# A two-layer gated network on one core: the hand-written slot tables of the first full turn are changed

## The reference, cut to what matters

```python
q = batch_norm(x1 @ w_q)                            # x1 is the output of the attention
sim = einsum('pbnhd,hkpd->pbnhk', q, keys)          # 8 heads, 2 halves, 32 keys each
sx, ix = top_k(sim[0], 8);  sy, iy = top_k(sim[1], 8)
scores, pk = top_k(sx[..., :, None] + sy[..., None, :], 8)
h = gelu(einsum('bnd,bnhkd->bnhk', x1, down_embed[indices]))
out = einsum('bnhk,bnhkd->bnd', softmax(scores) * h, up_embed[indices])
x2 = x + out
# second layer: h1 = relu(x2n @ W1 + b1); h2 = relu(h1 @ W2 + b2); c = sum_e cw_e (h2 @ W3 + b3)
# then gelu(c @ W1f + b1f) @ W2f + b2f, weighted by the two best of 8 sigmoid gates, and x3 = x2 + that
```

## Time and profile before

| what | value |
|---|---|
| median of 3 runs | 784.82 us (784.77 to 787.23) |
| profiled execution, its own time | 787.02 us |
| its span | 785.2 us |
| PE busy | 741.9 us (94%) |
| DVE busy | 557.1 us (71%) |
| ACT busy | 575.6 us (73%) |
| POOL busy | 312.2 us (40%) |
| mean granted clock of TensorE | 0.987 |

### The profile page before, as it was taken

One profiled execution on the slowest core, in us unless ns is written; L12 is line 12 of the kernel. 1 busy time (PEld: TensorE's weight loads), 2 busy tenths in 40 slices (PEclk: granted clock), 3 DMA queues, 4 the chain that ended last, 5 costly groups with the idle time before them and its releaser, 6 DMA issues.

```text
span 785.2 us, 14852 instructions
## 1 busy us (share of the span) xinstructions
PE 741.9 (94%) x5314; PEld 654.1 (83%) x5314; DVE 557.1 (71%) x1495; ACT 575.6 (73%) x1001; POOL 312.2 (40%) x214
## 2 busy tenths in 40 slices
PE   6889998979878999999999999999999999999998
PEld 4666767869766799899989989999898899999887
DVE  4887888477379877976977797688679756833422
ACT  3677777369797778978987886897889788553243
POOL 2122222179977175344717543572645161000000
PEclk9999999989997999999999999999999999999999
DMA  8940000000000000000000000000000000000000
GB/s 313 333 117 2 3 1 2 1 1 1 1 1 1 1 1 8 2 1 2 7 1 2 8 1 1 1 8 1 1 5 4 1 1 8 1 1 8 1 1 8
DMA packets 11160, 16.92 MB, mean 22 GB/s; under 512 B 680, under 2 KB 6992, under 8 KB 10832
## 3 DMA queue, kind: packets, MB, share of 16 engines
q1 hardware_dynamic: 10944, 15.72, 6.2%
q10 hardware_dynamic: 144, 0.26, 0.1%
HBM read 14.93 MB, written 1.05 MB: 20 GB/s over the span
## 4 chain that ended last, share of the span: by engine, by line
PE 85%; DVE 6%; ACT 4%; issue 3%; DMA 1%; SPq 0%; DVEq 0%; ACTq 0%
PE banks L448 79%; PE banks L484 4%; ACT G_both L936 2%; PE banks L695 2%; DVE W_both L1444 1%; DMA region<-in_pA 1%; ACT region L1014 1%; DVE acc L1589 1%; PE banks L512 1%; DVE W_both L1213 0%; DVE HF L1450 0%; ACT region L1020 0%; PE banks L727 0%; DVE pairs L1408 0%; DVE top_keys L1403 0%
## 5 line engine op out<-in xcount | busy, mean ns | idle before, releaser
L390 POOL TENSOR_TENSOR region<-sim 128x1024 f32<-128x1024 f32 x128 | 260.8, 2065 | 100.1 <-DVE top_keys L1401 63.2
L1076 ACT ACTIVATE HF<-banks,lpack 128x256 f32<-128x256 f32 x256 | 105.4, 479 | 55.6 <-PE banks L448 54.6
L1014 ACT ACTIVATE region<-region,neg_thr 128x1024 f32<-128x1024 f32 x128 | 143.8, 1153 | 0.0
L1444 DVE SCALAR_TENSOR_TENSOR W_both<-region,rz_rel,W_both 128x1024 f32<-128x1024 f32 x98 | 138.1, 1409 | 1.7
L448 PE MATMUL banks<-HF,w_sb 128*128 128x256 f32 x512 | 124.7, 388 | 7.7 <-DVE HF L1450 7.6
L448 PEld LDWEIGHTS banks<-f_sb,HF 128*128 128x128 f32 x1024 | 123.7, 192 | 3.4
L1020 ACT ACTIVATE region<-region,dtop 128x1024 f32<-128x1024 f32 x114 | 125.3, 1141 | 0.0
L448 PE MATMUL banks<-f_sb,HF 128*128 128x128 f32 x1024 | 124.5, 275 | 0.0
L448 PE MATMUL banks<-cT,f_sb 128*128 128x256 f32 x512 | 122.7, 382 | 0.1
L448 PEld LDWEIGHTS banks<-HF,w_sb 128*128 128x128 f32 x512 | 95.4, 194 | 20.0 <-DVE HF L1450 8.6
L448 PEld LDWEIGHTS banks<-cT,f_sb 128*128 128x128 f32 x512 | 92.1, 190 | 16.3 <-issue 2.9
(11 more groups left out here) (167 smaller groups left out, 1032.7 us busy)
## 6 DMA issues: line engine op xcount, KB each, us to landing
w_sb<-in_w SPq DMA_DIRECT2D x1, 2048.0 KB, 14.0
f_sb<-in_f SPq DMA_DIRECT2D x1, 2048.0 KB, 15.8
region<-in_wq SPq DMA_DIRECT2D x1, 1024.0 KB, 7.9
region<-in_wqT SPq DMA_DIRECT2D x1, 1024.0 KB, 10.0
w_sb<-in_w SPq DMA_DIRECT2D x1, 1024.0 KB, 8.5
out_x<-acc_f SPq DMA_DIRECT2D x16, 64.0 KB, 1.6
x1T_all<-in_xT SPq DMA_DIRECT2D x1, 768.0 KB, 7.7
region<-in_pA SPq DMA_DIRECT2D x1, 588.5 KB, 6.3
```

The lines of the kernel that those rows point to most:

```text
L390: pool.tensor_tensor(S[a][h].rearrange("p (i j) -> p i j", i=NK), sim[a][:, h, :].unsqueeze(2).broadcast_to([P, NK, NK]), sim[a][:, PH + h ...
L1014: act.activation(S[a][h], S[a][h], ACT.Prelu, bias=neg_thr[t % 4][:, h:h + 1], alpha=STEEP).then_inc(h_L, 1)
L1076: m = act.activation(HF[e % 2][:, f, :], bank(2 + b, 256 * (f % 2), 256 * (f % 2) + 256), ACT.Gelu_apprx_tanh, bias=L("bf", 4 * e + f, 4 * ...
L1444: v.scalar_tensor_tensor(W[a], S[a][h], rz_rel[a][:, h:h + 1], W[a], ALU.mult, ALU.add).then_inc(h_w, 1)
```

## The change

Only tables of turn 1 and turn 2 change, on ACT and DVE; turns from 3 on use the tables they used. PE and POOL have the same instructions in the same order.

- In turn 1 DVE searches tile 4 two slots later: `key_sums` and `top_keys_of` (slot 1) stand behind slot 8 rather than slot 6, `pair_sums` and `top_pairs` (slot 2) behind slot 9 rather than 7, `thresholds` (slot 3) behind slot 10 rather than 8.
- In turn 1 the sum of head 7 moves from slot 9 to 10. Of tile 3's seven sums (heads 9 to 15) four stood before slot 12 and one stands there now; the other six follow in the slots 12 to 15.
- In turn 1 ACT takes the steep steps of head 14 in slot 10 and 15 in slot 11 (before 9 and 10), and those of tile 4's heads 0 to 2 (16 to 18) in the slots 13 and 14 (before 10 and 11); the rest of tile 4's follow. The exponentials of the heads 13 to 15 move with them (13 from slot 9 to 10, 15 from 10 to 11).
- The exponentials of tile 4's heads 0 to 2 move from slot 11 of turn 1 into slot 4 of turn 2. There ACT's table is now `EXPS_2`, and the sums of tile 4's heads 1 and 2 leave the slots 0 and 2 (`SUMS_2`).

```diff
--- before.py
+++ after.py
@@ -1106,14 +1106,15 @@
             EXPS = {4: [3, 4, 5, 6], 5: [7], 6: [8], 7: [9, 10], 8: [11], 9: [12, 13], 10: [14, 15], 11: [17, 18]}
             STEEPS = {0: [7, 8], 1: [9], 2: [10, 11, 12], 3: [13], 6: [14], 7: [15], 8: [16], 9: [17], 10: [18],
                       13: [19], 14: [20], 15: [21, 22]}
-            STEEPS_1 = {0: [2], 1: [3], 4: [4, 5], 5: [6], 6: [7, 8], 7: [9, 10], 8: [11, 12], 9: [13, 14], 10: [15, 16],
-                        11: [17, 18], 13: [19], 14: [20], 15: [21, 22]}
-            EXPS_1 = {0: [2], 4: [3, 4], 5: [5], 6: [6, 7], 7: [8, 9], 8: [10, 11], 9: [12, 13], 10: [14, 15], 11: [16, 17, 18]}
+            STEEPS_1 = {0: [2], 1: [3], 4: [4, 5], 5: [6], 6: [7, 8], 7: [9, 10], 8: [11, 12], 9: [13], 10: [14],
+                        11: [15], 13: [16, 17], 14: [18, 19], 15: [20, 21, 22]}
+            EXPS_1 = {0: [2], 4: [3, 4], 5: [5], 6: [6, 7], 7: [8, 9], 8: [10, 11], 9: [12], 10: [13, 14], 11: [15]}
+            EXPS_2 = {4: [0, 1, 2, 3], 5: [4, 5], 6: [6, 7], 7: [8, 9], 8: [10, 11], 9: [12, 13], 10: [14, 15], 11: [17, 18]}
 
             def turn(g, peer, new, old, more=True):
                 t, G1, G2 = 2 * g, g - 1, g - 2
                 late = new and g > 1
-                steeps, exps = (STEEPS, EXPS) if late else (STEEPS_1, EXPS_1)
+                steeps, exps = (STEEPS, EXPS_2 if g == 2 else EXPS) if late else (STEEPS_1, EXPS_1)
 
                 def heads(s, at, do):
                     for h in at.get(s, []):
@@ -1622,15 +1623,17 @@
 
             SUMS = {0: [1], 2: [2], 4: [3], 6: [4], 7: [5], 8: [6], 9: [7], 10: [9, 10], 11: [11, 12], 12: [13],
                     13: [14], 14: [15]}
-            SUMS_1 = {0: [1], 6: [2, 3], 7: [4], 8: [5], 9: [6, 7], 10: [9, 10], 11: [11, 12], 12: [13], 13: [14], 14: [15]}
+            SUMS_1 = {0: [1], 6: [2, 3], 7: [4], 8: [5], 9: [6], 10: [7], 11: [9], 12: [10, 11], 13: [12, 13], 14: [14], 15: [15]}
+            SUMS_2 = {4: [1], 5: [2], 6: [3, 4], 7: [5], 8: [6], 9: [7], 10: [9, 10], 11: [11, 12], 12: [13],
+                      13: [14], 14: [15]}
             ADDS = {6: 0, 7: 1, 8: 2, 9: 3, 10: 4, 11: 5, 14: 8, 15: 9}
             OLD_ADDS = {0: 10, 1: 11, 2: 12, 3: 13}
 
             def turn(g, peer, new, old, more=True):
                 t, G1, G2 = 2 * g, g - 1, g - 2
                 late = new and g > 1
-                sums = SUMS if late else SUMS_1
-                slots = list(range(16)) if g != 1 else [4, 5, 0, 6, 1, 7, 2, 8, 3, 9, 10, 11, 12, 13, 14, 15]
+                sums = (SUMS_2 if g == 2 else SUMS) if late else SUMS_1
+                slots = list(range(16)) if g != 1 else [4, 5, 0, 6, 7, 8, 1, 9, 2, 10, 3, 11, 12, 13, 14, 15]
                 for s in slots:
                     if s == 4 and new:
                         mean_square(G1)
```

## The result

The changed kernel took 788.15 us (median of 18 executions, 786.24 to 790.88) beside 785.89 us for the kernel before; the ratio is 1.0028 with a 95% interval of 1.0015 to 1.0040. That is 2.2 us on 784.82 (1.0028 x 784.82 = 787.0), where 787.5 was forecast: the kernel is slower by about 0.3%. One of the 18 executions of the kernel before took 2618.2 us and the others 784.51 to 787.35; the ratio is that of the fast runs alone.

The account below looks back on a forecast made before the run. PE was taken to bound from turn 2 on, with DVE holding PE up in turn 1. Terms -0.3 + 0.5 + 2.5 = +2.7 us on the median 784.82 gave 787.5 us; the 8-in-10 range was 782.4 to 790.0.

Parts of the forecast that it names:

- A: Turn 1, slots 7 to 12: sum_T 2.6 us earlier, 2.3 lost to the lowered clock; -0.3 us, bounds -3.7 to +1.6.
- What bounds the kernel: PE bounds from turn 2 on; up to about 15 us lie in turn 1, where PE waits mostly for DVE.
- The cost of a DVE row beside POOL: A sum or pair table waits for the running POOL step's end, 0 to 1.9 us; rows reading PSUM don't.
- C: Turn 2, slots 4 to 12: two more DVE sums and waits for POOL make it +2.5 us, bounds +0.6 to +4.5.
- the walk: DVE's rows timed one by one: turn 1's seventh sum ends at 253.1 us; turn 2's sum_T is 2.6 us late.
- B: Turn 1, slots 12 to 15: ACT's additional steep steps delay gelus that PE needs; +0.5 us, bounds 0 to +1.5.
- The lower bound: Turn 2, slots 4 to 12: two sums of 2.5 us less 1.2 and 0.7 of slack, +0.6 us.
- Turn 1 wins more: Rival, 17%: turn 1 gains 3.1 us without clock loss, its end costs 0, turn 2 costs 0.6; -2.5, 782.3 us.
- They cancel: Rival, 22%: POOL's steps fall favourably in turn 2, +1.2; turn 1 gives -1.5, its end +0.3; 784.8 us.
- The clock falls in turn 2 too: Rival, 12%: waits from hidden2(4) on lower turn 2's clock for some 4 us of work, another 2.0; +4.7, 789.5 us.

Follow-up runs that it names:

- e9_pool_later: Changed kernel with one POOL wait raised, so no POOL step starts between turn 2's two sums in a row in slot 6; 788.71 us, 1.0026 of the kernel before.
- e4_sums67: Changed kernel with turn 1's sum of head 7 back in slot 9 and the search's second half behind slot 10; 784.73 us, 0.9977 of the kernel before.
- e3_steeps: Changed kernel with ACT's steep step of tile 4's head 2 in slot 13 instead of 14 of turn 1; 787.62 us, 1.0010 of the kernel before.
- e6_turn2_only: Kernel before with only ACT's tables and turn 2's sums of the change, DVE's turn 1 as it was; 788.75 us, 1.0034 of the kernel before.
- e1_spread: Changed kernel with turn 2's sums of tile 4's heads 4 to 6 each one slot later; 788.87 us, 1.0031 of the kernel before.
- e2_spread_late: As e1_spread, with turn 2's sums of tile 5's heads 10 to 12 also moved into slot 12; 786.15 us, 0.9995 of the kernel before.
- e8_short_sums: Changed kernel with the sums of tile 4's heads 1 and 2 done on 64 of 1024 columns; 785.85 us, 0.9994 of the kernel before.
- e5_sums_only: Kernel before with only tile 3's sums later in turn 1 (heads 10 to 15 in slots 12 to 15); 787.43 us, 1.0010 of the kernel before.

## Why the prediction was right

The sign, the size (2.7 us forecast, 2.2 timed, 1.84 in the stretches) and the range held, and within them two of the three terms; the third, A, was too small by 1.4 us, inside its stated bounds.

- *What bounds the kernel.* Right: all differences lie in turns 1 and 2, and turn 3 is unchanged (35.54 and 35.59 before its G).
- *The cost of a DVE row beside POOL.* Right and shown by e9_pool_later (4.35 to 2.66). The Trainium skill's rule ("SBUF — State Buffer", section "Who interferes with whom") agrees with this pair of numbers, and of the two values that the prediction gives for term C, 2.5 with waiting and 0.6 without, the first is the nearer to the 2.94 measured. The other half of the rule, as the prediction tells it, does not hold as it stands: the copy of the two best has one SBUF input, and it took 1.31 us at 307.58, to the end of the POOL step of 306.95, and 0.17 us at 266.91 in the kernel before with POOL idle; the threshold row at 250.22, also with one, took 1.88. The section limits that half to instructions outside the two-port modes and counts copies among those that can enter them. The prediction's walk let this copy and the thresholds wait all the same.
- *A, turn 1.* Right in mechanism, too small: -1.66 measured, -0.3 forecast. The seventh sum ended at 250.30, or 252.5 on the clock of the kernel before, where the walk said 253.1; `weights_T` came 1.30 us earlier instead of 0.7. PE's gap before it was 5.41 us (5.9 forecast). `sum_T` was forecast near 264.0 and came at 262.7 on that clock. Of the 1.4 us that A was off, 0.6 is this and 0.8 the clock: 10.09 us from `weights_T` to `sum_T` instead of the 8.6 without it, so 1.5 us where 2.3 was taken from the earlier stall. (The same products take 8.32 us in turn 2 of the kernel before, at full clock and without a wait; by that the clock cost 1.8.) e4_sums67 shows what the gap was worth: with it down to 1.23 us, T1 is 4.1 us shorter.
- *B, the end of turn 1.* Right: +0.51 for +0.5, e3_steeps takes it away, and e6_turn2_only shows it alone.
- *C, turn 2.* Right: +2.94 for +2.5, the wait of 1.7 us before `hidden2(4)` forecast and 1.73 measured, the pair of sums forecast at 1.2 and 3 us and measured at 4.35 together. The reading behind it was incomplete in two points. The lower bound counted 1.9 us of DVE's slack as free for the new sums; but DVE now stands idle for 1.09 us before `hidden1(1)` (300.81), ahead of them, and only about 0.8 us of it was used. As an estimate from DVE's rows, with what each takes beyond the shortest of its kind in these profiles, the waiting beside POOL in this stretch grew from 3.5 to 4.8 us, so that C is 2.5 (two sums) + 1.3 - 0.8 = 3.0. And the walk treats the POOL step as the thing to avoid, and e1_spread and e9_pool_later show that removing it at one place only moves the waiting (by the same estimate 4.8 and 4.9 us in these two), since DVE has no slack left up to `sum_T`; what helped was work taken away from there (e2_spread_late, e8_short_sums).
- *The rivals.* "Turn 1 wins more" fails: the gap was there, and turn 2 cost 2.9, not 0.6. "They cancel" had A right (-1.5 against -1.66) but not C (+1.2). "The clock falls in turn 2 too" did not happen in the profile: it was granted in full (1.00) from 296.7 to 334.6. The reason that the prediction gives against it, that 1.7 us is well under 4.36, was weaker than it looks: in the kernel before the row at 246.02 (3.47 us for eight products) stands behind a wait of 2.06 us, and the clock was at 0.50 from 247 to 249.

One thing in the comparison isn't settled: the timed ratio is 2.2 us, the stretches say 1.84. The difference lies within the interval (1.2 to 3.1 us). The fastest executions, 786.24 and 784.51, are 1.7 us apart. That the timed number came as near to the forecast as it did is partly luck, since term A was off by 1.4 us one way and term C by 0.4 the other.

## What to carry to other kernels

When work is moved off a busy engine, look for the one instruction that another engine waits for next and count what now stands ahead of it: here three sums left DVE, and the seventh sum of the tile still came late, as half a search had been put before it; moving that sum one slot forward and that half search one slot back was worth 4.1 us. Where an engine had no slack left up to a deadline (DVE in turn 2), two reorderings of what lies before it brought nothing (e1_spread, e9_pool_later); putting three sums behind it brought 2.0 us. Measure from mark to mark in the traces when an edit is worth less than the spread of the whole time.

## What the runs showed of the hardware that was not expected

- The same instructions ahead of turn 1 took from 210.95 us (e3_steeps) to 213.81 us (e1_spread) in the profiles, with the granted clock at half in other places: in the kernel before from about 171 to 178 us, in the changed kernel from about 172.5 to 175.5. Behind turn 3's G it was 414.7 to 414.8 us in ten of them and 416.3 and 416.4 in e5_sums_only and e1_spread. The changed kernel's 18 executions fall into groups by their mean granted clock: 786.2 to 787.0 us at 0.987 to 0.991, 788.1 to 788.6 at 0.985, and 789.6 to 790.1 at 0.980 (one, 790.88, at 0.982). So a median depends on how many executions fall into which group; why one execution gets one and not the other is open.
- Stalls of PE of 2.02 us (e5_sums_only), 2.06 us (the kernel before at 246.02) and 2.15 us (the changed kernel at 232.72) were followed by products at half the clock; the wait of 1.73 us in turn 2 was not.
- DVE's waiting beside POOL in turn 2 up to `sum_T` came to the same 4.8 to 4.9 us (the estimate above) in the changed kernel, e1_spread and e9_pool_later, though it stood at different rows.
